# A decoder of two layers on one core: the work of the last cross-attention units and of the first expert half put in another order

## The reference

```python
x = x + L0_attn(norm(x)); x = x + L0_xattn(ctx, norm(x)); x = x + L0_ffn(norm(x))
x = x + L1_attn(norm(x))
# fifth: cross attention, 16 heads, keys and values from ctx (4, 256, 64)
q_big = rope(einsum('bshk,hkq->bshq', (x @ Wq.T).reshape(B, S, 16, 128), w_kc_q))
kv_r = rope(kv_c)
scores = einsum('bhsr,bhlr->bhsl', q_big @ W_qr, kv_r @ W_kr)
ctx = softmax(scores) @ kv_r            # then w_kc_kv, then Wo
# sixth: 16 experts of 176 rows, 6 chosen per token, and a shared expert of 352
probs = softmax(x @ gate_w.T); top 6, normed to sum 1
out = sum_e combine[e] * (silu(x @ w1g[e].T) * (x @ w1u[e].T)) @ w2[e].T
out = out + shared expert, without a router weight
```

## Time and profile before

| | |
|---|---|
| median of 3 runs | 896.26 us (895.15 to 899.03) |
| the profiled execution's own time | 897.05 us |
| its span in the profile | 895.0 us |
| mean granted clock of PE | 0.994 |
| PE busy | 869.9 us, 97% |
| DVE busy | 619.2 us, 69% |
| ACT busy | 430.5 us, 48% |
| POOL busy | 98.1 us, 11% |
| cross units | from 447.6 us to about 676 us |
| expert stage of layer 1, second half of tokens first used | 691.72 us |

### The profile page before, as it was taken

One profiled execution on the slowest core, in us unless ns is written; L12 is line 12 of the kernel. 1 busy time (PEld: TensorE's weight loads), 2 busy tenths in 40 slices (PEclk: granted clock), 3 DMA queues, 4 the chain that ended last, 5 costly groups with the idle time before them and its releaser, 6 DMA issues.

```text
span 895.0 us, 13929 instructions
## 1 busy us (share of the span) xinstructions
PE 869.9 (97%) x5281; PEld 669.3 (75%) x5281; DVE 619.2 (69%) x1154; ACT 430.5 (48%) x1079; POOL 98.1 (11%) x79
## 2 busy tenths in 40 slices
PE   8998999999999999999989999999979999999998
PEld 5665778888888876767767777767657788888886
DVE  4669756666665756667778888889757666666665
ACT  7554543434343468883344444445365443344342
POOL 4001000000000150000321323223200000000000
PEclk9999999999999999999999999999999999999999
DMA  7003111111100410013100000000201111111001
GB/s 192 1 2 126 36 53 49 40 53 53 35 0 1 178 76 1 2 71 129 68 1 1 1 2 1 1 1 1 89 18 37 53 37 53 53 49 39 18 1 47
DMA packets 12535, 37.33 MB, mean 42 GB/s; under 512 B 2080, under 2 KB 4352, under 8 KB 11712
## 3 DMA queue, kind: packets, MB, share of 16 engines
q1 hardware_dynamic: 12448, 36.58, 12.6%
q0 software_dynamic: 32, 0.01, 0.0%
HBM read 35.54 MB, written 1.05 MB: 41 GB/s over the span
## 4 chain that ended last, share of the span: by engine, by line
PE 84%; DVE 8%; ACT 5%; issue 2%; POOL 1%; DVEq 0%; ACTq 0%; POOLq 0%
PE ps L1437 78%; PE ps L2083 3%; PE ps L1610 2%; DVE probs_q L931 1%; DVE P L586 1%; ACT Q L1200 1%; ACT probs_q L1332 1%; POOL outer_rot L1430 1%; DVE rope_buf L865 1%; DVE xn L518 1%; ACT DT L1017 1%; DVE stats L510 1%; DVE wlo L852 0%; DVE neg_max L921 0%; ACT h_hi L1245 0%
## 5 line engine op out<-in xcount | busy, mean ns | idle before, releaser
L1245 ACT ACTIVATE h_hi<-weighted_h 128x512 fp32r<-128x512 f32 x100 | 63.2, 632 | 150.3 <-DVE weighted_h L736 148.1
L746 DVE TENSOR_TENSOR h_lo<-weighted_h,h_hi 128x512 fp32r<-128x512 f32 x100 | 69.2, 692 | 66.1 <-ACT h_hi L1245 65.9
L1437 PE MATMUL ps<-xT_second,whi 128*128 128x512 f32 x376 | 108.5, 391 | 0.2 <-ACT silu_g L1240 0.2
L1437 PE MATMUL ps<-xT_first,whi 128*128 128x512 f32 x376 | 108.6, 390 | 0.0
L773 DVE TENSOR_TENSOR shared_gate<-silu_g,row_shares 128x512 f32<-128x512 f32 x88 | 60.9, 692 | 61.9 <-ACT silu_g L1240 61.6
L1240 ACT ACTIVATE silu_g<-ps 128x512 f32<-128x512 f32 x100 | 59.7, 598 | 73.4 <-PE ps L1437 73.4
L1437 PEld LDWEIGHTS ps<-xT_second,whi 128*128 128x128 f32 x376 | 70.1, 188 | 15.6 <-issue 1.1
L1437 PEld LDWEIGHTS ps<-xT_first,whi 128*128 128x128 f32 x376 | 70.3, 188 | 15.1 <-issue 0.5
L1332 ACT ACTIVATE probs_q<-ps,neg_max 128x256 f32<-128x256 f32 x128 | 58.7, 485 | 45.9 <-DVE neg_max L921 45.9
L1437 PE MATMUL ps<-h_hi,wlo 128*128 128x512 f32 x200 | 78.0, 390 | 0.0
L1437 PE MATMUL ps<-h_hi,whi 128*128 128x512 f32 x188 | 74.2, 395 | 0.4 <-DVE h_lo L746 0.3
(11 more groups left out here) (212 smaller groups left out, 1652.4 us busy)
## 6 DMA issues: line engine op xcount, KB each, us to landing
raw<-in_ffn SPq DMA_DIRECT2D x50, 384.0 KB, 3.0
wx<-in_wx SPq DMA_DIRECT2D x4, 2112.0 KB, 8.1
cx<-in_cx SPq DMA_DIRECT2D x1, 1536.0 KB, 6.4
X<-in_x SPq DMA_DIRECT2D x4, 256.0 KB, 7.1
kvc<-in_kvc SPq DMA_DIRECT2D x1, 1024.0 KB, 14.3
out<-X SPq DMA_DIRECT2D x4, 256.0 KB, 2.2
wqkv<-in_wqkv SPq DMA_DIRECT2D x1, 768.0 KB, 8.5
wqkv<-in_wqkv SPq DMA_DIRECT2D x1, 512.0 KB, 6.2
```

The lines of the kernel that those rows point to most:

```text
L746: v.tensor_tensor(h_lo[:, u % 2, :], weighted_h[:, u % 2, :], h_hi[:, u % 2, :].bitcast(F32), ALU.subtract).then_inc(act_lo[l], 1)
L1245: a.activation(h_hi[:, u % 2, :], weighted_h[:, u % 2, :], ACT.Copy).then_inc(act_hi[l], 1)
L1437: return pe.matmul(o, l, r, start=start, stop=stop, skip_group_check=True)
```

## The change

It has four parts.

1. The first ropes and norms of the probabilities: `rope(6)` stands ahead of the loop and not behind the row maxima of unit 0, and in unit 0 the second half of the norm (`normalise_probs(0, 1)`) comes behind `operand_rest(1)`.
2. The layer norm's steps inside the loop (units 8 to 11) stand behind `operand_rest(w+1)`, and not ahead of it.
3. The end of the cross stage. The turning of tokens 0 to 511 is taken apart and goes into units 12 and 13, with its copies and subtractions. The router's logits and the first gate go into unit 14, the second gate and the first up into unit 15, second up, third gate and first down before `tokens_turned(1, 1)`. The first weight splits go into units 13 and 14. The router logits of the second half of tokens come last, after `down_half(1)`. The waits change with that: `output(11)` and `output(12)` wait for the subtraction of the turned tokens, which now use their bank 7.
4. Banks and buffers: the first gates, ups and turned tokens of layer 1 use other banks, and in the SBUF map of the cross stage `neg_max`, `sums` and `rsum` stand ahead of `kvl`, `tSh` and `tSl`, with a hole for the router's tiles.

```diff
--- the vector engine's list
                 operand_rest(0)
+                rope(2 * CHUNKS_PER_UNIT)
                 for w in range(UNITS):
...
                     if more:
-                        rope(ahead)
+                        if w >= 1:
+                            rope(ahead)
                         rope(ahead + 1)
-                    elif w == UNITS - 1:
-                        split_lo(1, 0, 0)
...
                     normalise_probs(w, 0)
-                    normalise_probs(w, 1)
+                    if w >= 1:
+                        normalise_probs(w, 1)
+                    if w in (UNITS - 4, UNITS - 3):
+                        tokens_low(1, 0, (w - UNITS + 4,))
+                    if w == UNITS - 3:
+                        split_lo(1, 0, 0)
+                    if w == UNITS - 2:
+                        router_maxima(1, 0)
+                        split_lo(1, 1, 1)
+                        split_lo(1, 2, 2)
+                    if w + 1 < UNITS:
+                        operand_rest(w + 1)
+                    if w == 0:
+                        normalise_probs(w, 1)
                     if w in (2 * GROUPS, 2 * GROUPS + 1):
                         norm_statistics(5, w - 2 * GROUPS)
                     if w in (2 * GROUPS + 2, 2 * GROUPS + 3):
                         normalise(5, w - 2 * GROUPS - 2)
-                    if w + 1 < UNITS:
-                        operand_rest(w + 1)
-                tokens_low(1, 0)
                 copy_transposed(UNITS - 1)
-                split_lo(1, 1, 1)
+                weight_shared(1, 0)
                 add_output(UNITS - 2)
+                act_low(1, 0, 0)
                 norm_statistics(5, NB - 2)
-                split_lo(1, 2, 2)
                 normalise(5, NB - 2)
+                weight_shared(1, 1)
+                router_probabilities(1, 0)
                 add_output(UNITS - 1)
                 norm_statistics(5, NB - 1)
-                router_maxima(1, 0)
+                act_low(1, 1, 1)
                 normalise(5, NB - 1)
-                weight_shared(1, 0)
                 tokens_low(1, 1)
-                router_probabilities(1, 0)
-                act_low(1, 0, 0)
-                weight_shared(1, 1)
                 router_choice(1, 0)
-                act_low(1, 1, 1)
--- the scalar engine's list
                 for w in range(UNITS):
                     exponentials(w, 0)
+                    if w == UNITS - 2:
+                        copy_logits(1, 0)
                     exponentials(w, 1)
+                    if w in (UNITS - 4, UNITS - 3):
+                        tokens_high(1, 0, (w - UNITS + 4,))
+                    if w == UNITS - 1:
+                        logit_exponentials(1, 0)
                     if w >= 1:
                         copy_transposed(w - 1, 0)
                         copy_transposed(w - 1, 1)
                         if w == UNITS - 1:
-                            tokens_high(1, 0)
+                            silu(1, 0, 0)
                         contexts(w - 1)
                     if w in (2 * GROUPS + 1, 2 * GROUPS + 2):
                         norm(5, w - 2 * GROUPS - 1)
+                    if w == UNITS - 3:
+                        split_hi(1, 0, 0, 0)
+                    if w == UNITS - 2:
+                        split_hi(1, 1, 1, 0)
+                        split_hi(1, 2, 2, 0)
                     if w + 1 < UNITS:
                         operand_high(w + 1)
-                    if w == UNITS - 2:
-                        split_hi(1, 0, 0, 0)
+                silu(1, 1, 1)
                 copy_transposed(UNITS - 1, 0)
                 copy_transposed(UNITS - 1, 1)
-                split_hi(1, 1, 1, 0)
-                split_hi(1, 2, 2, 0)
+                act_high(1, 0, 0)
+                a.preload_act_table_set(LN_EXP)
                 contexts(UNITS - 1)
                 norm(5, NB - 2)
+                act_high(1, 1, 1)
                 spread_rows(1)
-                copy_logits(1, 0)
                 norm(5, NB - 1)
-                logit_exponentials(1, 0)
-                silu(1, 0, 0)
                 tokens_high(1, 1)
-                silu(1, 1, 1)
-                act_high(1, 0, 0)
                 silu(1, 2, 2)
                 copy_logits(1, 1)
-                act_high(1, 1, 1)
--- the tensor engine's list
+                    if w in (UNITS - 5, UNITS - 4):
+                        pe.wait_ge(xt_lo, 4 + w - UNITS + 6)      # in output(w)
...
-                    elif w == UNITS - 1:
-                        tokens_turned(1, 0)
+                    elif w == UNITS - 2:
+                        pe.wait_ge(rope_products, 2 * LATENT_CHUNKS)
+                        router_logits(1, 0)
+                        gate_half(1, 0, 0, False, 0)
+                    else:
+                        pe.wait_ge(logits_shifted, 2 + 1)
+                        gate_half(1, 1, 0, False, 1)
+                    if w in (UNITS - 4, UNITS - 3):
+                        pe.wait_ge(*output_added(w - 2))
+                        turned_half(1, 0, w - UNITS + 4)
                     if w >= 1:
                         transposed_probabilities(w - 1, 0)
                     if more:
                         latent_queries(ahead + 2)
+                    elif w == UNITS - 2:
+                        logits_by_token(1, 0)
+                    else:
+                        up_half(1, 0, 0, False, 0)
...
                 output(UNITS - 2)
                 weighted_contexts(UNITS - 1)
-                router_logits(1, 0)
+                up_half(1, 1, 0, False, 1)
                 output(UNITS - 1)
-                logits_by_token(1, 0)
-                gate_half(1, 0, 0, False, 0)
-                up_half(1, 0, 0, False, 0)
-                gate_half(1, 1, 0, False, 1)
+                gate_half(1, 2, 0, False, 2)
+                down_half(1, 0, 0, False, 0)
                 tokens_turned(1, 1)
-                gate_half(1, 2, 0, False, 2)
-                up_half(1, 1, 0, False, 1)
-                router_logits(1, 1)
-                down_half(1, 0, 0, False, 0)
                 up_half(1, 2, 0, False, 2)
                 down_half(1, 1, 0, False, 1)
+                router_logits(1, 1)
```

More of the change, by code:

```diff
@@ L413, in next_split, with gate_bank, up_bank @@
             return u // 2 + 2
-        def gate_bank(n):
-            return 2 * (n - 1) if isinstance(n, int) and n in (1, 2) else 4
+        def gate_bank(l, n):
+            if l == 1 and isinstance(n, int) and n < 2:
+                return n
+            return 2 * (n - 1) if l == 0 and isinstance(n, int) and n in (1, 2) else 4
+        def up_bank(l, n, u):
+            return 2 if l == 1 and isinstance(n, int) and n == 0 else 5 + u % 2
         def y_bank(t):
@@ L725, in turned_keys, with tokens_low @@
                     v.tensor_scalar(half[:, b].rearrange("p m s -> p (m s)"), ps[:, turn_bank(b) + 1, :], k(sign), None, ALU.mult).then_inc(k_turned, 1)
-            def tokens_low(l, hf):
-                for kk in range(KD):
+            def tokens_low(l, hf, kks=range(KD)):
+                for kk in kks:
                     v.wait_ge(xt_hi, 4 * l + 2 * hf + kk + 1)
@@ L1215, in split_hi, with tokens_high @@
                 a.activation(high_weights(l, c // RING if isinstance(c, int) else c, slot)[:, slot, :], (raw0, raw1)[l][:, slot, :], ACT.Copy).then_inc(w_hi[l], 1)
-            def tokens_high(l, hf):
-                for kk in range(KD):
+            def tokens_high(l, hf, kks=range(KD)):
+                for kk in kks:
                     a.wait_ge(pe_ffn_xt, 4 * l + 2 * hf + kk + 1)
@@ L1871, in gate_half @@
                     pe.wait_ge(xt_hi, 2)
-                three(gate_bank(n), high_weights(l, i, slot), slot, 0, hf, 2 if l == 0 and isinstance(n, int) and n == 0 else 0).then_inc(pe_gate_part[l], 1)
+                three(gate_bank(l, n), high_weights(l, i, slot), slot, 0, hf, 2 if l == 0 and isinstance(n, int) and n == 0 else 0).then_inc(pe_gate_part[l], 1)
             def up_half(l, n, i, last, u):
@@ L1878, in up_half @@
                     pe.wait_ge(weighted[l], n - 1)
[L1879 removed]
+                three(up_bank(l, n, u), high_weights(l, i, slot), slot, 256, hf).then_inc(pe_up_part[l], 1)
             def down_half(l, n, i, last, u):
                 slot, hf = half_chunk(i, last, u)
[L1883 removed]
+                if l == 0 and isinstance(n, int) and n == 0:
                     pe.wait_ge(silu_done[l], EARLY)
```

31 lines of the change are left out of this document (15 added, 16 removed).

## The result

The changed kernel takes 890.41 us (median of 5 runs, 889.83 to 891.15); the kernel before took 896.35 us beside it (895.15 to 899.3). The medians are 5.9 us apart; the estimated ratio is 0.9926 with the 95% interval [0.9903, 0.9948]. The forecast was 891.0.

A forecast was written before the change was run, and what follows sets the result against it. PE's list, busy 97% of the span, was taken as the bound, so only its waits and low clock could be won. 3.3 + 0.8 - 2.1 + 4.5 - 1.3 = 5.2 us off 896.26 gave 891.0 us; 8-in-10 range 888.5 to 894.5.

The forecast's parts named there:

- Part 1: Units 0 to 2: earlier rope and later half norm cut PE's waits and the low clock; 3.3 us saved (1.5 to 3.8).
- Part 2: Units 8 to 11: norm steps behind tSl remove two tSl waits of odd units; 0.8 us saved (0.3 to 0.9).
- Part 3a: Units 12 and 13: eight transpositions move in (1.1 us) and a wait of 1.0 us arises; minus 2.1 us.
- Part 3b: Unit 14 to first second-half gate: 8.5 us go out, 4.0 of new waits come in; 4.5 us saved (2.5 to 6.5).
- New waits 4.0: Unit 14 to first second-half gate: PE waits of 0.95, 0.8, 1.6 (contexts) and 0.6 us (behind the last output).
- Part 3c: First experts: the router's choice ends later and delays silu(3), for which step 4's gate waits; minus 1.3 us (0 to 2.0).
- 1, the clock falls elsewhere: Rival, chance 0.22: PE's clock still falls, or falls elsewhere; 892.7 us with one fall, 894.5 with two.
- 2, DVE bounds the odd units: Rival, chance 0.13: added DVE work and moved norms delay odd units and double the late new waits; 893.5 us.
- 3, the drain of about 1380 ns: Rival, chance 0.05: table loads drain ACT at the contexts and silu(3), 1.4 to 2.8 us more; 893.2 us.
- 4, the low clock from unit 14 on: Rival, chance 0.06: waits of units 13 to 15 and first experts keep the clock low; 30 us would give 906.
- 5, more won: Rival, chance 0.08: PE's new waits are half of those counted; 888.5 us.

The follow-up runs named there:

- The experiment: Changed kernel with the token subtraction of unit 13 ahead of the rope for the next query half: 889.41 us, ratio 0.9928; unit 13 14.92 us (16.03).
- The reordering: Changed kernel with silu(3) ahead of the router's exponential on ACT and the router's choice behind act_low(3) on DVE: 889.1 us, ratio 0.9905.
- after_again: The changed kernel itself, nothing altered, run again on the same chip as three of the follow-up kernels: 890.66 us, ratio 0.9942.
- first_only: Kernel before with only rope(6) ahead of the loop and the second half norm of unit 0 behind tSl: 893.24 us, ratio 0.9962.
- fill_gaps: Kernel before with 23 added matmuls whose result nobody reads, in three gaps of PE in units 0, 1 and 14: 894.32 us, ratio 0.9966.

## Why the prediction held

**Part 1.** The steps came as worked out. The maxima start late by little, there is no wait on rope_buf, the half norm beside POOL took 2.25 us (2.2 assumed), and unit 2 starts at 471.74 (471.4), 23.50 us behind unit 0 (23.8). The wait on tSl is 1.53 us where the kernel before had 2.03, though PE comes 1.5 us earlier. What the forecast took for granted was that the fall of the clock belongs to the kernel. It came in one of four profiles with those waits. The 1.4 us of it are won only against an execution that has it; the lasting gain of the stage is 2.2 us, where the sum had 3.3. The 3.55 us of the table come from the one profile of before that had the fall, so that the match there is luck. The forecast also priced a fall by the share that the window lost (1.8 and 1.7 us); the units say 15.66 - 14.28 = 1.38 and 14.67 - 13.08 = 1.59.

**Part 2.** Both waits on tSl, ahead of units 10 and 12, are gone: 0.95 us (0.8).

**Part 3a.** Unit 13 took 16.03 us (15.8), with a wait of 1.23 us (1.0), and it stands ahead of output(12), as the working had it. The weight split there never waited for its transfer: ACT began it at 638.95, as the copy of contexts ended. The experiment adds that the price was one of order: 1.1 of the 2.2 us can be had back.

**Part 3b.** Here a term was mis-sized: "New waits 4.0". They are 0.58, 0.61 and 1.36 us, and 0.35 us behind the last output: 2.9 in place of 0.95 + 0.8 + 1.6 + 0.6. The last of them isn't in the list of PE's waits. It sits inside the turning of the second half of tokens, whose weight loads (PEld) wait for DVE's norm, so that the row takes 1.38 us where it took 1.03 before:

```profile
679.44 1.38 PE L1836 MATMUL ps<-cst,xn 128*128 128x128 f32 x8
679.73 0.14 PEld L1836 LDWEIGHTS ps<-cst,xn 128*128 128x128 f32 x1 [0.15 <-DVE xn L527]
680.05 0.53 PEld L1836 LDWEIGHTS ps<-cst,xn 128*128 128x128 f32 x5 [0.19 <-DVE xn L527]
```

DVE from the last output added to that norm, with `act_low` (`h_lo`) in between:

```profile
676.97 0.69 DVE L950 TENSOR_TENSOR X<-X,ps 128x512 f32<-128x512 f32 x1 [0.36 <-PE ps L1458]
...
678.58 0.66 DVE L755 TENSOR_TENSOR h_lo<-weighted_h,h_hi 128x512 fp32r<-128x512 f32 x1
679.26 0.74 DVE L527 TENSOR_SCALAR xn<-X,mv,rstd 128x256 f32<-128x256 f32 x2
```

The norm starts 2.3 us behind the add, exactly as before (678.64 to 680.94 in the earlier trace rows), though `act_low` came in. The estimate took the 3.0 us from add to the norm's end as fixed and added `act_low`. But those 3.0 us held the `router_maxima` of the first half (0.19 and 0.22 us at 680.25 and 680.48), which the change itself moves away, and 0.23 us of idle time; `act_low` took their place.

With that the stage closes. The waits are 1.1 us shorter than forecast and the stage saved 1.0 us more. The 0.1 us between them is the fall of the clock, counted at 1.7 and measured at 1.59. Against the two further profiles of before, whose fall is cheaper, the stage (45.08 and 44.87 us) saved only 4.9 and 4.6 us. Of that 4.1 us lie behind the start of unit 15, which takes 31.04 to 31.08 us to the gate in every profile with the old end, and 26.97 with the new one.

**Part 3c.** The wait on silu(3) is 1.42 us (0.20 before), the stage 1.33 longer (1.3). The chain is the one forecast. Silu(2) ended at 683.4, but the product that needs it (`weighted_h`) started only as the router's choice (`comb`) ended, 1.2 us later, about what the wait grew by:

```profile
682.82 0.60 ACT L1256 ACTIVATE silu_g<-ps 128x512 f32<-128x512 f32 x1
```

```profile
684.47 0.22 DVE L857 TENSOR_TENSOR comb<-comb,softmax_den 128x64 f32<-128x64 f32 x1
684.61 0.68 DVE L745 TENSOR_TENSOR weighted_h<-ps,silu_g 128x512 f32<-128x512 f32 x1
```

Behind it ACT went through `act_high(2)`, the split, a load, the exponential and a load to silu(3) at 689.74. The reordering took 1.6 us back, more than the change had cost.

**The rivals.** 1, the clock falls elsewhere: no. In both profiles of the changed kernel it is 1.00 in every window of 10 us from 90 us on. 2, DVE bounds the odd units: no. Only unit 13 of them has a new wait, 1.23 us, and the order made it. 3, the drain of about 1380 ns that the Trainium skill, ScalarE: Activation LUTs, What ACT_TABLE_LOAD costs, adds to a table load: no. Loads of 1.28 us at 665.49 and 688.44 are followed by silu at 666.78 and 689.74, 0.01 to 0.02 us behind their ends. Here the measurement decides. 4, the low clock from unit 14 on: no. 5, more won: in part, in 3b.

**What the median owes to chance.** Before ran from 894.65 to 901.22 us over all batches, the changed kernel only from 889.83 to 891.15. The gain between medians (5.9 us, and 5.0 in the batch of after_again, whose interval reaches beyond the 0.5% bound) thus holds a share of falls of the clock that come in some executions only. Between the lowest times, 894.65 and 889.83, it is 4.8 us, and from unit 0 to the gate of step 4 the two further profiles of before take 4.3 us more than the changed kernel (246.6 on average, 242.24). So against an ordinary execution of before the change gives 4.3 to 4.8 us, 5.2 was forecast, and that the medians came out so near it, at 5.9, is in part luck: the forecast overpriced the falls of the clock, it overpriced the new waits, which works the other way, and it knew nothing of the long executions of before.

The mean granted clock of each execution says what the long ones are. It was under 0.995 in 18 of the 40 executions of before on the two chips of the experiments, and in 4 of the 12 of first_only, its four slowest (895.55 to 896.67 us, the others at most 893.29). It was 0.995 or more in all 59 executions of kernels that have no wait over 0.8 us in unit 14: fill_gaps and every kernel with part 3. So the long executions are low clocks too, and in these runs they went with the wait of unit 14, not with the early ones. Two falls of some 1.5 us don't make 901 us, so there must be more of them; where they lie isn't shown, since none of these executions has a profile.

## What to carry to other kernels

Put an instruction that another engine waits for ahead, in its own engine's list, of work that nobody waits for yet: a subtraction ahead of a rope, a copy ahead of a table load, a silu ahead of the router's loads. Three such moves brought 3.2 us on top of the change, without removing an instruction. When work is moved into a gap, sum what is then in front of each waited-for instruction (queue by queue), as this forecast did. The stage sums were right within 0.3 us except in one stage, where a copied duration held idle time and work that the change itself took away: look at what a duration is made of before carrying it over. A clock fall seen in one profile is a sample: take two or three more, and the granted clock of every execution, before its cost enters a sum, and price it by the stage and not by the window.

## What the hardware did that was not expected

- The same waits of PE, 1.47 and 2.03 to 2.06 us within 7 us, were followed by the lower of the two clock levels in one execution of four, at 1.4 us; the wait of 2.19 us in unit 14 was followed by it in four of four (0.93 over 636 to 662 us in each). The four falls cost 0.75 to 1.59 us, since a low clock ahead of a wait is partly hidden by the wait.
- Executions with a mean granted clock under 0.995 came only in kernels with that wait of 2.19 us: 22 of 52, against none of 59 without it.
- Matmuls that nobody reads, put in these gaps, shortened the kernel by 2.3 us between medians, 0.8 us between profiles without the early fall.
- A table load costs ACT its 1.28 us and no more; the next instruction of ACT started 0.01 to 0.02 us behind its end in the rows shown, and 0.12 us once (688.17), where it waited for DVE's logits of 687.91.
- Four VectorE scalings of 128x256 f32 took 1.14 us alone (at 640.53), 2.25 us in unit 0 and 3.25 us in unit 13, where POOL was adding beside them for 1.3 and 2.6 us of that time (its rows start at 453.23 and 637.12).
